# One product per block with the parts selected afterwards, and quad-wise pooled products, in a windowed linear-attention kernel

## The reference, cut to what matters

```
qkv = einsum('nchw,oc->nohw', xw, qkv_w)          # 384 channels
pooled = avg_pool5(qkv)                           # inside the 4x4 window
msq = concat([qkv, pooled], 1) -> (window, 32 heads, 16 pixels, 3*8)
q, k = relu(msq[..., :8]), relu(msq[..., 8:16])
v = pad(msq[..., 16:], one column of 1)           # 9 columns
kv = einsum('ngld,nglm->ngdm', k, v)              # 8 x 9 per head and window
out = einsum('ngld,ngdm->nglm', q, kv)            # 16 x 9
out = out[..., :8] / (out[..., 8:] + 1e-15)
y = einsum('nchw,oc->nohw', out, proj_w), batch norm
return x + y
```

## Time and profile before

| | us |
|---|---|
| median of 3 runs | 887.09 |
| lowest, highest | 884.8, 888.21 |
| the profiled execution, time | 886.18 |
| its span | 884.3 |
| PE busy | 848.4 |
| DVE busy | 699.9 |
| POOL busy | 658.9 |
| ACT busy | 480.9 |

### The profile page before, as it was taken

How to read it: one execution, slowest core, us unless ns; L and a number is a source line. 1 busy time by engine, 2 the same in 40 slices (tenths; PEclk the granted TensorE clock), 3 DMA queues, 4 the chain that set the end, 5 groups by cost and what they waited for, 6 DMA issues and landing times.

```text
span 884.3 us, 63772 instructions
## 1 busy us (share of the span) xinstructions
PE 848.4 (96%) x28322; PEld 693.0 (78%) x28322; DVE 699.9 (79%) x1252; ACT 480.9 (54%) x1349; POOL 658.9 (75%) x1624
## 2 busy tenths in 40 slices
PE   0789999999999999999999999999999999999997
PEld 0568888888888888888888888888888888888885
DVE  7758888887778888888777888888777777777776
ACT  0346565646465655555555556565656564646563
POOL 2558787878787878777878777787878787878781
PEclk9999999999999999999999999999999999999999
DMA  6122322111123323111113232211111111111111
GB/s 236 40 77 81 103 84 82 49 47 48 47 69 97 91 94 98 51 48 47 49 50 99 86 98 88 82 51 48 48 50 46 49 48 47 48 47 48 47 49 47
DMA packets 39081, 60.06 MB, mean 68 GB/s; under 512 B 8560, under 2 KB 33648, under 8 KB 39024
## 3 DMA queue, kind: packets, MB, share of 16 engines
q1 hardware_dynamic: 39024, 59.52, 20.0%
HBM read 19.38 MB, written 18.87 MB: 43 GB/s over the span
## 4 chain that ended last, share of the span: by engine, by line
PE 94%; DVE 3%; issue 1%; DMA 1%; SPq 0%; ACT 0%; DVEq 0%
PE ps L703 24%; PE ps L687 17%; PE ps L659 14%; PE ps L668 9%; PE ps L675 9%; PE ps L787 7%; PE ps L778 6%; PE ps L789 4%; PE ps L676 4%; DVE stats L453 1%; DMA x_all<-x 0%; DVE kvc_full L561 0%; DVE kvc_pool L561 0%; DMA vm_full<-v_full 0%; DVE kvc_full L509 0%
## 5 line engine op out<-in xcount | busy, mean ns | idle before, releaser
L366 ACT ACTIVATE vm_pool<-ps,cst 128x256 f32<-128x256 f32 x576 | 230.1, 480 | 0.0
L376 ACT ACTIVATE q_full<-ps 128x384 f32<-128x384 f32 x96 | 47.2, 491 | 281.0 <-PE ps L675 281.0
L561 DVE TENSOR_TENSOR kvc_full<-ps,cst 128x864 f32<-128x864 f32 x192 | 193.2, 1048 | 4.7 <-PE ps L687 4.7
L561 DVE TENSOR_TENSOR kvc_pool<-ps,cst 128x864 f32<-128x864 f32 x192 | 193.2, 1048 | 0.5 <-PE ps L687 0.5
L286 POOL TENSOR_TENSOR xd<-x_all,mean_t 128x384 f32<-128x384 f32 x95 | 78.6, 827 | 154.3 <-PE ps L676 137.8
L659 PE MATMUL ps<-wkv_sb,xn 128*128 128x256 f32 x576 | 141.4, 382 | 23.1 <-DVE xn L517 23.1
L264 POOL TENSOR_TENSOR x_all<-y_pool,x_all 128x96 f32<-128x96 f32 x380 | 148.9, 424 | 12.7 <-DVE x_all L567 7.2
L659 PEld LDWEIGHTS ps<-wkv_sb,xn 128*128 128x128 f32 x576 | 109.4, 191 | 33.2 <-issue 23.0
L703 PEld LDWEIGHTS ps<-kvc_full,q_full 64*32 64x32 f32 x9216 | 108.3, 105 | 26.0 <-issue 26.0
L292 POOL TENSOR_TENSOR xn<-xd,rstd_t 128x96 f32<-128x96 f32 x380 | 121.8, 367 | 8.1 <-DVE xn L517 0.7
L703 PE MATMUL ps<-kvc_full,q_full 64*32 64x72 f32 x9216 | 125.0, 230 | 0.6 <-DVE kvc_pool L561 0.6
(11 more groups left out here) (74 smaller groups left out, 1316.2 us busy)
## 6 DMA issues: line engine op xcount, KB each, us to landing
vm_full<-v_full SPq DMA_DIRECT2D x384, 54.0 KB, 1.9
out<-x_all SPq DMA_DIRECT2D x96, 192.0 KB, 1.9
x_all<-x SPq DMA_DIRECT2D x36, 384.0 KB, 3.4
x_all<-x SPq DMA_DIRECT2D x6, 768.0 KB, 7.9
cst<-consts SPq DMA_DIRECT2D x1, 170.0 KB, 11.0
wkv_sb<-wkv SPq DMA_DIRECT2D x1, 128.0 KB, 10.8
o_sb<-proj SPq DMA_DIRECT2D x1, 128.0 KB, 10.1
wq_sb<-wq SPq DMA_DIRECT2D x1, 64.0 KB, 10.6
```

The costliest lines, as they stand in the source:

```text
L366: last = act.activation(heads[:, e, :, :, 0:D], src, ACT.Copy, scale=col(C_VP + e))
L561: last = dve.tensor_tensor(kvc[:, g], src.to_broadcast(shape), own, ALU.mult)
```

## The change

- Full `out_products`: a block's q stands in `q_full` once, both windows side by side. One matmul has the kv of both windows as its right-hand side (144 columns), so its output holds, for every pixel, the product with its own window's kv and with the other's. 24 matmuls instead of 48. The block's wanted part is chosen afterwards on DVE: `select(s)` copies the part of window 0 for all rows (`tensor_copy`) and then overwrites the rows of window 1 (`copy_predicated` with a mask from the constants).
- Pooled: likewise one matmul for three windows, and each is over one quad (32 rows) instead of two quads with masks. `out_pooled(s, 0)` takes the first quad of each half, `out_pooled(s, 1)` the second, 16 matmuls of 108 columns each; the first stands ahead of the full products, the second behind them and behind a wait for the first (`half_out_p`). These use the array as 32 rows by 32 columns. `select_pooled(s)` is one copy and two `copy_predicated`.
- `kvc_pool` then needs only a head mask. ACT makes it with four activations (`own_heads_pooled`), DVE no longer does.
- `divide(s)` is one for both branches, from `sel` in SBUF, followed on DVE by `own_heads(s + 1)`.
- `conv_q(s+1)` stands between the full and the pooled kv products.
- PSUM banks, semaphores and some places on ACT (`pooled_out` behind `relu_k`) follow. `transposes` now waits for `num` (the divide), `qm_f` and `kvc_p`; `kv_products` for `y_copied`; the pooled `conv_q` for `vm_p`; `kv_products_pooled` for `sel_f`.

```diff
+        q_full = sb("q_full", [TF * 4, Q4])
+        q_pool = sb("q_pool", [TP * 4, Q4])
+        kvc_pool = sb("kvc_pool", [G, HALF, KC])
+        sel = sb("sel", [G, TF + TP, QG * KC])
...
+            def own_heads_pooled(s):
+                act.wait_ge(kv_p, s + 1)
+                wait(act, out_p, s)
+                src = ps[:, KVP:KVP + G, 0:HALF * KC].rearrange("p g (w c) -> p g w c", c=KC)
+                for h in range(4):
+                    cols = slice(h * HC, (h + 1) * HC)
+                    last = act.activation(kvc_pool[:, :, :, cols], src[:, :, :, cols], ACT.Copy,
+                                          scale=col(C_HEAD + h))
+                last.then_inc(kvc_p, 1)
...
+            def select(s):
+                dve.wait_ge(out_f, s + 1)
+                wait(dve, num, s)
+                dve.tensor_copy(sel_f_part, full_windows(0)).then_inc(win_f, 1)
+                dve.wait_ge(win_f, s + 1)
+                dve.copy_predicated(sel_f_part, rows_of(1, [P, G, TF, QG * KC]), full_windows(1)).then_inc(sel_f, 1)
+            def select_pooled(s):
+                dve.wait_ge(out_p, s + 1)
+                dve.tensor_copy(sel_p_part, pooled_windows(0)).then_inc(win_p, 1)
+                dve.wait_ge(win_p, s + 1)
+                for e in range(1, WP):
+                    dve.copy_predicated(sel_p_part, rows_of(WF + e, [P, G, TP * QG, KC]),
+                                        pooled_windows(e)).then_inc(sel_p, 1)
+                    dve.wait_ge(sel_p, (WP - 1) * s + e)
...
             def step(s, b, at, phase):
-                own_heads(s, False)
...
-                own_heads(s, True)
+                if not is_first(s):
+                    residual(s - 1)
+                select(s)
+                select_pooled(s)
+                divide(s)
+                if not is_last(s):
+                    own_heads(s + 1)
...
-            def out_tile(pooled, t, e, full_bank=OUTF):
+            def out_tile(t):
...
                     for c in range(4):
...
+                        last = pe.matmul(ps[Q4 * c:Q4 * (c + 1), OUTF + g, t * n:(t + 1) * n],
+                                         q_full[rows, 4 * t + c], kvc_full[rows, r, w:w + WF],
+                                         start=True, stop=True)
+            def pooled_out_tile(t, j):
...
+                    rows, at = slice(H64 * g + Q4 * j, H64 * g + Q4 * (j + 1)), (t * QG + j) * n
...
                 if not is_first(s):
-                    project(s - 1, out_next=True)
+                    project(s - 1)
+                out_pooled(s, 0)
                 out_products(s)
-                out_products_pooled(s)
+                out_pooled(s, 1)
                 kv_products(s + 1)
+                conv_q(s + 1, p)
                 kv_products_pooled(s + 1)
-                conv_q(s + 1, p)
```

More of the change, by code:

```diff
@@ L549, in link, with own_heads @@
                 dve.wait_ge(dv, s * DV + n)
[L551 to L556, removed]
+            def own_heads(s):
+                dve.wait_ge(kv_f, s + 1)
+                wait(dve, out_f, s)
                 shape = [P, HALF, QG, KC]
@@ L584, in residual_pooled_last, with rows_of @@
                 last.then_inc(y_done, 1)
[L586 to L590, removed]
-                src = ps[:, bank:bank + G, 0:tiles * QG * KC].rearrange("p g (n c) -> p g n c", c=HC)
-                link(dve.tensor_scalar(den[:], src[:, :, :, D], DEN_EPS, None, ALU.add), s, step + 1)
-                link(dve.reciprocal(den[:], den[:]), s, step + 2)
-                wait(dve, turned, s)
-                heads = [P, G, tiles * QG * 4, D]
+            def rows_of(window, shape):
+                return col(C_WIN + window).bitcast(mybir.dt.uint32).unsqueeze(2).unsqueeze(3).to_broadcast(shape)
@@ L596, in divide @@
+            def divide(s):
+                dve.wait_ge(sel_f, s + 1)
+                src = sel[:].rearrange("p g t (h c) -> p g (t h) c", c=HC)
+                link(dve.tensor_scalar(den[:], src[:, :, :, D], DEN_EPS, None, ALU.add), s, 1)
+                link(dve.reciprocal(den[:], den[:]), s, 2)
+                wait(dve, tr_p, s)
+                heads = [P, G, (TF + TP) * QG * 4, D]
                 dve.tensor_tensor(o[:].rearrange("p t (h m) g -> p g (t h) m", m=D), src[:, :, :, 0:D],
-                                  den[:].unsqueeze(3).to_broadcast(heads), ALU.mult).then_inc(done, 1)
+                                  den[:].unsqueeze(3).to_broadcast(heads), ALU.mult).then_inc(num, 1)
@@ L644, in _ @@
             dve.tensor_copy(projT[:], ps[:, TRF, 0:2 * P]).then_inc(projT_ready, 1)
+            own_heads(0)
             over_strips(step)
@@ L754, in out_products_pooled, with out_products, transposes @@
+            def out_products(s):
+                pe.wait_ge(kvc_f, G * (s + 1))
+                pe.nop(nofuse=True)
+                for t in range(TF):
+                    last = out_tile(t)
+                last.then_inc(out_f, 1)
+            def transposes(s):
+                pe.wait_ge(num, s + 1)
+                if not is_last(s):
+                    pe.wait_ge(qm_f, s + 2)
                 else:
                     pe.wait_ge(added_f, s)
-                    pe.wait_ge(y_copied, s)
@@ L782, in project @@
-            def project(s, out_next=False):
+                for t in range(TF):
+                    last = pe.transpose(ps[:, TRF, t * P:(t + 1) * P], o[:, t].rearrange("p c g -> p (c g)"),
+                                        col(C_IDENT, P))
+                last.then_inc(tr_f, 1)
+                if not is_last(s):
+                    pe.wait_ge(kvc_p, s + 2)
+                pxs = 4 * WP * PXP
+                for t in range(TP):
+                    last = pe.transpose(ps[:, TRP, t * pxs:t * pxs + P], o[:, TF + t].rearrange("p c g -> p (c g)"),
+                                        col(C_PACK, P))
```

163 lines of the change are left out of this document (72 added, 91 removed).

## The result

The changed kernel takes 951.9 us (951.02 to 952.39, 4 runs) against 887.6 us, a ratio of 1.073 (1.0705 to 1.0755): slower, by more than the forecast of 903 us and outside the range given. Its span is 949.7 us.

What follows compares the result with a forecast made beforehand. PE alone was taken as the bound: a strip goes from 8.77 to 8.91 us, 93 periods add 13 us and the end 3, so 886.2 + 16 = 902.2 profiled, 903 us measured; range 850 to 912.

Steps and rivals of the forecast that it cites:

- PE's groups of a strip: Sum of PE's group costs from projection to projection: 8.91 us, against 8.77 before the change.
- changes between small arrays, three: On PE, switches between 32-row and 64-row small arrays around the out products: each stops PE 0.17 us.
- out products to `num` on DVE: DVE's chain of selecting instructions, sum, reciprocal and product after the full out products: 4.33 us together.
- PE's wait for that chain, a strip: Before the transposes: none, since they can start at 4.54 us and PE reaches them at 4.95, cover 0.41.
- end of the program, more: After the last strip the whole DVE chain of 4.3 us stands open, less 0.5 of matmuls: some 3 us.
- What bounds the kernel before: Whole loop: PE, busy 96%, without idle time before its groups; 93 periods of 8.77 us.
- PE part by part: PE's groups: shorter out products save 0.73 us a strip, moved q convolutions cost some 0.37, three small-array changes 0.17 each.
- The change on the others, and why I cost it at nothing: DVE, ACT, POOL and queues: DVE's divide hidden by 0.41 us, ACT's copies by 0.08, POOL and queues unchanged.
- one sum of 80 denominators 0.24 + 0.03: In DVE's chain before the reciprocal: the sum over 80 denominators was priced at 0.24 + 0.03 us.
- Rival (b): DVE's predicated copies take two passes; PE waits 0.64 us before every transpose, 963 us; chance 0.12.
- Rival (a): On PE, small arrays of two heights follow without a stop: 8.40 us a strip, 856 us; chance 0.24 in full.
- Rival (c): ACT's four masked copies or another thin cover fails by 0.1 to 0.2 us a strip: 912 to 922 us; chance 0.06.

Runs made afterwards that it cites:

- e2: Changed kernel, but DVE's sum of 80 denominators reads meaningless numbers in PSUM instead of SBUF; right denominators left out: 907.8 us, ratio 1.0241.
- e4: As e3, but complete: ACT writes pooled q twice, each time with the other quad zeroed, so nothing is left out: 905.9 us, ratio 1.0225.
- e1: Changed kernel with one wait added: GpSimd starts a strip's normalisation only after the divide; nothing left out: 908.3 us, ratio 1.025.
- e3: e1 with 64 rows instead of 32 in the pooled out products; separation of the two quads left out: 905.8 us, ratio 1.0229.
- e9: e4 with two of the four DMAs that spread v left out, so v of two windows in four is missing: 894.1 us, ratio 1.0098.
- e8: Kernel before the change, with two of the four DMAs that spread v issued by ACT instead of SP: 1010.4 us, ratio 1.1378.

## Why the prediction was wrong

| term | forecast, us | measured, us |
|---|---|---|
| PE's groups of a strip | 8.91 | 6.10 + 1.40 + 1.41 = 8.91; a strip of e2 8.94 (median) to 8.98 (mean) |
| changes between small arrays, three | 0.17 each | 0.53 - 0.39 = 0.14 and 0.92 - 0.74 = 0.18 (e4) |
| out products to `num` on DVE | 4.33 | 708.51 - 703.30 = 5.21 |
| PE's wait for that chain, a strip | none, 0.41 of cover | about 0.5 (9.45 against 8.94 to 8.98) |
| end of the program, more | 3 | 22.35 - 17.21 = 5.1 |
| start of the program, more | not in the sum | 48.10 - 45.59 = 2.5 |
| time | 903 | 951.9 |

The loop is longer by 93 x (9.454 - 8.834) = 57.7 us; with 5.1 and 2.5 that is 65.3 of the 65.4 us between the two spans.

- **What bounds the kernel before** was read right: PE alone. What I did not read is how near the next bounds lay. I looked for waits and there were none; the 0.2 us between the DMAs' landing and the full kv products show only if one adds 3.8 us to the end of v's copy.
- **PE part by part** was right in sign and size. The full and the pooled products become shorter by what the columns say, the stops eat it, and the moved q convolutions cost about 0.4. e1 and e2, where the failed term is gone, are 21 us over the kernel before; my sum said 16, and the difference lies at the start and the end. The Trainium skill's rule that changing the tiling mode drains the engine ("TensorEngine Tiling (Array Packing)", Tiling Modes) held for small arrays of two heights as well: e4 against the changed kernel shows 0.14 to 0.18 us per change.
- **The step that failed** is "The change on the others, and why I cost it at nothing", and in it the term "one sum of 80 denominators 0.24 + 0.03". It was 0.89 + 0.03. The product was 0.91 instead of 0.83, and the selecting instructions together 0.14 longer. The chain came to 5.21 instead of 4.33 us, 0.88 more against a cover of 0.41: PE waits about 0.5 us before every transpose. I took the duration from a row whose source was PSUM and used it for one in SBUF, and I looked on DVE's timeline for what precedes and follows the instruction, not on GpSimd's for what lies beside it. In the loop this is 93 x (9.45 - 8.98) = 44 us, as much as e1 gives back in all, 43.7.
- The Trainium skill states this on "SBUF — State Buffer", Who interferes with whom: a VectorE `tensor_scalar` may run in a mode that uses a port pair shared with GpSimd, whoever comes first keeps the pair for its whole instruction, and a VectorE instruction with two SBUF inputs contends with GpSimd's reads. The trace agrees: 0.24 us from PSUM and 0.88 from SBUF beside the same 0.83 us subtraction, 0.91 against 0.83 for the product. It agrees on the order too: where the sum came first it took 0.23 and the subtraction 0.90. Applied to the two moved operands the rule would have put up to 0.65 + 0.08 us on the chain, against a cover of 0.41: a wait of 0.3 us a strip, 30 us in the loop, which is an estimate and less than was measured. That GpSimd's subtraction would start just at the sum's moment no row of the kernel before could say.
- **Rival (b)** named the right place, DVE's chain, with a price near the truth (963) and the wrong mechanism: the predicated copies take one pass, 658 against 608 ns for 432 elements.
- **Rival (a)**, 856 us, could not have come true even without stops: e3 and e4 have none and take 906, held by the DMAs. It assumed that PE's sum would be the strip. Its remark that the divide's cover would shrink to 0.15 us points at what e9 shows: there the chain is 4.70 us on the mean instead of 4.33, and PE waits for it.
- **Rival (c)** did not occur in the loop: in e2 the kvc copies end 0.09 us before the pooled transposes start, as thin as forecast (0.08). PE waits for them there once each in e3 and e4, for 0.15 us, behind the loop.
- The end of the program was put at 3 us and is 5.1. That term was mis-sized: besides the last strip's 4.06 us, where 0.65 were, PE waits 1.06 us for `o` in the strip before it, where it waited 0.43, since no k and v convolution stands in front of those transposes any more to cover the chain.

Of the 0.06 us a strip between e1's mean (9.00) and its median (8.94), 0.04 are four waits for the DMAs that spread v, 3.7 us together. What stays open is the later start of the loop, 2.5 us, and why those four landings were late.

## What to carry to other kernels

When a change moves an operand from PSUM to SBUF, its duration has to be read again beside the engine that shares the memory's way: lay the timelines of VectorE and GpSimd over each other, not only the instruction's neighbours in its own queue. Not every instruction pays: the reciprocal, in SBUF as well, did not. When the bound is removed by a change, compute for every releaser how early it is, DMAs included (end of the producer, issues one behind another, landing); a cover of 0.2 us leaves no wait in the trace, and is gone with the first gain. And matmuls of another tile height between others cost a stop on each side: a zeroed operand that keeps the height was worth 0.15 us on each border here.

## What the runs showed of the hardware that I had not expected

- A VectorE sum over 80 elements waits out the GpSimd instruction that started before it when its source is SBUF (0.88 us beside 0.83, 0.46 to 0.50 beside additions of 0.4), and takes 0.24 us when it is PSUM. Whichever starts first is not held: 0.23 us for the sum when it led by 0.02 us, and 0.90 for the subtraction behind it.
- GpSimd pays too: one multiplication that starts during VectorE's product of two SBUF inputs takes 0.95 instead of 0.36 us. The reciprocal, SBUF to SBUF, neither pays nor costs: 0.65 us, with multiplications of 0.36 beside it.
- Two DMA issues on ACT keep its next activation 1.50 us behind the last one; two issues on SP take 1.10 us (e8).
- The stop at a change between small arrays of two heights is of the size of that between small arrays and the whole one: 0.14 to 0.18 us (e4 against the changed kernel), stagger included, beside 0.18 on leaving the small arrays in the kernel before.
